# Cross-attention block on one Trainium2 core: the feed-forward as seven block products in two passes over F

## The reference, cut to what matters

```python
def _forward(query, context, wq, wk, wv, bq, bk, bv, wo, bo, ln1_g, ln1_b, ln2_g, ln2_b, w1, b1, w2, b2):
    ...
    o = jnp.einsum('bhqk,bkhd->bqhd', probs, vh).reshape(Bq, Sq, Dm)
    attn_out = o @ wo + bo
    x = query + attn_out
    h = _layer_norm(x, ln2_g, ln2_b)
    ff = jax.nn.gelu(h @ w1 + b1, approximate=False) @ w2 + b2
    return x + ff
```

## Time and profile before

| | |
|---|---|
| median of three runs | 3067.84 us |
| the profiled execution, its own time | 3068.4 us |
| its span, first to last instruction | 3066.7 us |
| mean granted TensorE clock | 0.989 |
| TensorE busy (matmul) | 2944.3 us, 96% |
| VectorE busy | 1517.7 us, 49% |
| ScalarE busy | 1155.7 us, 38% |
| stage b, from its first instruction at 1559 us | about 1508 us |

### The profile page before, as it was taken

How to read it: one execution, slowest core, us unless ns; L and a number is a source line. 1 busy time by engine, 2 the same in 40 slices (tenths; PEclk the granted TensorE clock), 3 DMA queues, 4 the chain that set the end, 5 groups by cost and what they waited for, 6 DMA issues and landing times. The chain is left out here.

```text
span 3066.7 us, 52560 instructions
## 1 busy us (share of the span) xinstructions
PE 2944.3 (96%) x17576; PEld 2390.1 (78%) x17576; DVE 1517.7 (49%) x4100; ACT 1155.7 (38%) x2958; POOL 459.3 (15%) x432
## 2 busy tenths in 40 slices
PE   6999999999999999999879999999999999999999
PEld 5777877777777778777768888888888888888887
DVE  4776667766677666677534333322333322333322
ACT  3665666656666655666522111111111111111111
POOL 1221122212222211222122000000000000000000
PEclk9999999999999999999979999999999999999999
DMA  5766666766676666667431111110111110111100
GB/s 134 124 118 107 108 110 109 123 115 101 116 110 115 116 114 108 107 112 116 73 112 57 42 41 41 41 41 0 41 41 41 41 41 0 41 41 41 41 28 14
DMA packets 123695, 231.89 MB, mean 76 GB/s; under 512 B 10752, under 2 KB 10752, under 8 KB 123648
## 3 DMA queue, kind: packets, MB, share of 16 engines
q1 hardware_dynamic: 123648, 231.28, 37.9%
HBM read 97.02 MB, written 33.55 MB: 43 GB/s over the span
## 5 line engine op out<-in xcount | busy, mean ns | idle before, releaser
L711 ACT ACTIVATE sm<-sm,mins 128x128 f32<-128x128 f32 (+3 forms) x1024 | 571.7, 559 | 570.0 <-DVE mins L574 567.4
L574 DVE CUSTOM_DVE_ANT_0 sm<-bank_s,mask 128x128 f32<-128x128 f32 (+3 forms) x1024 | 480.4, 488 | 419.9 <-PE bank_s L425 409.4
L1148 ACT ACTIVATE g_sb<-bank_f,b1s 128x512 f32<-128x512 f32 x256 | 176.2, 688 | 1173.0 <-PE bank_f L958 1173.0
L1060 DVE CAST g_hi<-g_sb 128x512 fp32r<-128x512 f32 x256 | 113.1, 442 | 866.2 <-ACT g_sb L1148 866.1
L437 PE MATMUL bank_t<-ident,sm 128*128 128x128 f32 x2560 | 419.1, 278 | 72.2 <-DVE pT L520 37.2
L437 PEld LDWEIGHTS bank_t<-ident,sm 128*128 128x128 f32 x2560 | 299.5, 141 | 177.1 <-issue 59.2
L956 PE MATMUL bank_f<-hT_hi,w_hi 128*128 128x512 f32 x1024 | 407.5, 398 | 1.6 <-DVE hT_lo L1054 1.6
L956 PE MATMUL bank_o<-w_hi,g_hi 128*128 128x512 f32 x1024 | 408.0, 398 | 0.0
L958 PE MATMUL bank_f<-hT_hi,w_lo 128*128 128x512 f32 x1024 | 406.7, 397 | 0.0
L957 PE MATMUL bank_f<-hT_lo,w_hi 128*128 128x512 f32 x1024 | 406.3, 397 | 0.0
L958 PE MATMUL bank_o<-w_hi,g_lo 128*128 128x512 f32 x1024 | 406.3, 397 | 0.0
(11 more groups left out here) (108 smaller groups left out, 4457.6 us busy)
## 6 DMA issues: line engine op xcount, KB each, us to landing
stack<-st_hi SPq DMA_DIRECT2D x256, 256.0 KB, 6.0
xt<-in_x SPq DMA_DIRECT2D x32, 1024.0 KB, 5.3
stack<-st_lo SPq DMA_DIRECT2D x128, 256.0 KB, 7.3
c_raw<-in_ctxT SPq DMA_DIRECT2D x64, 256.0 KB, 6.1
x_scratch<-xt SPq DMA_DIRECT2D x64, 256.0 KB, 2.0
xn<-x_scratch SPq DMA_DIRECT2D x16, 1024.0 KB, 7.7
xr<-x_scratch SPq DMA_DIRECT2D x16, 1024.0 KB, 5.6
out<-xr SPq DMA_DIRECT2D x64, 256.0 KB, 2.1
```

The costliest lines, as they stand in the source:

```text
L574: op = V.tensor_tensor_reduce(sm[:, n % SLOTS_S, off:off + w], bank_s[n % BANKS_S][:, off:off + w], mask[:, 512 - w:512], 1.0, 0.0, ALU.ad ...
L711: op = A.activation(row, row, ACT.Exp, bias=mins[:, g % 2, c:c + 1], scale=-1.0, accum_out=sums[:, g % 2, c:c + 1])
L1060: V.tensor_copy(g_hi[:, f % RING_H, :], g_sb[:, f % 2, :]).then_inc(g_hi_ok, 1)
L1148: A.activation(g_sb[:, f % 2, :], bank_f[f % 2][:], ACT.Gelu, bias=b1s[:, f:f + 1], scale=1.0).then_inc(gelu, 1)
```

## The change

The feed-forward is done in two passes over F, 1024 columns each; all 16 sequences go through the first pass, then all through the second. In a pass both products are 2 x 2 block products done with seven block multiplications (Winograd's form) in place of eight. The weight sums (S1 to S4 of w1, T1 to T4 of w2) are made once for each pass, on VectorE, in place in the loaded buffers, and split like the rest. The input's sums (T1 to T4) are made once for each sequence in the first pass; the split parts (`b_hi`, `b_lo`, together 3.67 MB for a sequence) are stored to HBM and loaded back in the second pass.

Layer 1 (`layer1`): fourteen steps a pass (`STEPS`), seven for each half `d` of the hidden rows, 12 matmuls each, with 256 moving columns. Products are partly summed by copying a bank to SBUF while the bank goes on being summed into (`copy`: P1, P5, U2, on ScalarE), then adding on VectorE (`add`: C11, C12, C22); C21 goes from the bank to gelu.

Layer 2 (`layer2`): seven products `k` with two halves `h` of 12 matmuls of 256 columns. Its left operands are blocks of gelu's output or sums of them (`a_sum`: S1 to S4, on VectorE), then rounded on ScalarE (`a_high`) and the remainder taken on VectorE (`a_low`), in two buffers by `k % 2`; `a_high(k, h)` waits for half `h` of product `k - 2`. Results go to `xr` by `sum_out` on VectorE, into banks `bank_x2`, `bank_y2`, `bank_z2`.

In the first pass `xr` is the stage's input and is stored back to the scratch tensor; in the second pass it is read again, GpSimd adds b2, and the output is stored. The transposed input goes through three banks (`x_bank`), spread over the steps 8 to 11 of layer 1, and ScalarE applies the layer norm's scale and bias while it copies them out (`x_high`), so `bias_product` goes. ScalarE's order of a first-pass body ends in a `h_high` for each operand of the next sequence between the `a_high`; VectorE's order is in the diff. The weights of the first body of a pass are split inside that body (`w1_parts`, `w2_parts`: eleven VectorE instructions for each of four units); unit 3 is loaded into the same buffer `xr` as unit 2, after it is used, and the first body's `xr` only after unit 3 is used. `at(c, OUTPUTS, i)` waits until `i + 1` sums of the sequence are done, in whichever order VectorE makes them.

```diff
@@ -839,15 +839,44 @@
...
+
+
...
+    STEPS = [(0, 0), (0, 1), (0, 2), (0, 3), (0, 4), (0, 5), (1, 0), (0, 6),
+             (1, 1), (1, 2), (1, 3), (1, 4), (1, 5), (1, 6)]
+    X_AFTER = {8: 0, 9: 1, 10: 2, 11: 3}
...
         def sem(name):
             return ctx.enter_context(nc.semaphore(name))
 
-        w1_hi = sb("w1_hi", [P, KT, F], F32R)
...
+        def g_block(d, name):
+            rows, cols = "C1 C2".split().index(name[:2]), "12".index(name[2])
+            return g[:, 4 * d + 2 * rows:4 * d + 2 * rows + 2, C * cols:C * cols + C]
...
-
-
-            body(0, True, False)
...
+        def over_batches(eng, body):
+
+            body(0, 0, True, False)
             with eng.Fori(1, B - 1) as c:
...
+                body(c, 0, False, False)
+            body(B - 1, 0, False, True)
+            body(B, 1, True, False)
+            with eng.Fori(B + 1, 2 * B - 1) as c:
+                body(c, 1, False, False)
+            body(2 * B - 1, 1, False, True)
...
+            def b_view(b, part):
+                return b_scratch[bass.ds(b, 1)].rearrange("o h p n -> (o h) p n")[part]
...
+                    sp.wait_ge(stored, c * 32 + 32)
+                sp.dma_start(xr[:], one(x_v, b)).then_inc(xr_in, 16)
...
+                if ph == 0:
+                    sp.wait_ge(b_lo_ok, at(c, T_LOW, "T4"))
+                    for part, m in enumerate((b_hi, b_lo)):
+                        sp.dma_start(b_view(b, part), m[:].rearrange("p a k s -> p (a k s)").bitcast(F32)).then_inc(b_stored, 16)
...
+                if ph == 1 and not last or ph == 0 and last:
+                    sp.wait_ge(step1, at(c, STEPS, (1, 6)))
+                    sp.wait_ge(b_stored, 32 * B)
+                    for part, m in enumerate((b_hi, b_lo)):
+                        sp.dma_start(m[:].rearrange("p a k s -> p (a k s)").bitcast(F32),
+                                     b_view(0 if ph == 0 else b + 1, part)).then_inc(b_in, 16)
...
+                for half in range(2):
+                    sp.wait_ge(summed, at(c, OUTPUTS, 5 + half))
+                    sp.dma_start(one(to, b)[:, 2 * half:2 * half + 2, :],
+                                 xr[:, 2 * half:2 * half + 2, :]).then_inc(stored, 16)
...
-            def hidden(c, f):
...
-            def output(c, f):
...
-            def bias_product(wc, bank):
...
+            def block_product(o, lh, ll, rh, rl, opens):
+
+                pe.matmul(o, lh, rh, start=opens, stop=False, skip_group_check=True)
+                pe.matmul(o, lh, rl, start=False, stop=False, skip_group_check=True)
+                return pe.matmul(o, ll, rh, start=False, stop=True, skip_group_check=True)
...
+            def layer1(c, ph, first, d, at_place):
+                if first:
+                    w_ready(4 * ph + d, S_LOW, PLACE1_A[at_place])
+                if d == 0 and ph == 0:
+                    pe.wait_ge(b_lo_ok, at(c, T_LOW, PLACE1_B[at_place]))
...
+                    pe.wait_ge(b_in, (c - B) * 32 + 32)
+                bank = bank_x[d]
+                if at_place == 0:
+                    pe.wait_ge(gelu, before(c, GELUS, (d, "C21")))
+                if at_place == 1:
+                    bank = bank_y
+                    pe.wait_ge(added, before(c, ADDS, (1, "C12")) if d == 0 else at(c, ADDS, (0, "C12")))
+                if at_place == 2:
+                    bank = bank_z
+                    pe.wait_ge(added, before(c, ADDS, (1, "C11")) if d == 0 else at(c, ADDS, (0, "C11")))
+                if at_place == 3:
+                    pe.wait_ge(copied, at(c, COPIES, (d, "P1")))
+                if at_place == 4:
+                    bank = bank_y
+                    pe.wait_ge(copied, at(c, COPIES, (d, "P5")))
+                if at_place == 5:
+                    pe.wait_ge(copied, at(c, COPIES, (d, "U2")))
+                if at_place == 6:
+                    pe.wait_ge(added, at(c, ADDS, (d, "C22")))
+                for m in range(2):
+                    cols = slice(P * (2 * d + m), P * (2 * d + m) + P)
+                    for kt in range(2):
+                        mm = block_product(bank[:, C * m:C * m + C], w1_hi[:, at_place, kt, cols],
+                                           w1_lo[:, at_place, kt, cols], b_hi[:, at_place, kt, :],
+                                           b_lo[:, at_place, kt, :], at_place < 3 and m == 0 and kt == 0)
+                mm.then_inc(step1, 1)
...
+            def layer2(c, ph, first, k):
+                bank = bank_x2
+                if k == 0:
+                    pe.wait_ge(summed, before(c, OUTPUTS, 6))
+                if k == 1:
+                    bank = bank_y2
+                    pe.wait_ge(summed, before(c, OUTPUTS, 5))
+                if k == 2:
+                    pe.wait_ge(summed, at(c, OUTPUTS, 0))
+                if k == 3:
+                    bank = bank_z2
+                    pe.wait_ge(summed, before(c, OUTPUTS, 3))
+                if k == 4:
+                    pe.wait_ge(summed, at(c, OUTPUTS, 2))
+                if k == 5:
+                    bank = bank_y2
+                    pe.wait_ge(summed, at(c, OUTPUTS, 1))
+                if k == 6:
+                    pe.wait_ge(summed, at(c, OUTPUTS, 4))
+                for h in range(2):
+                    if first:
+                        w_ready(4 * ph + 2 + h, T_LOW, PLACE2_B[k])
+                    pe.wait_ge(a_lo_ok, at(c, A_LOW, (k, h)))
+                    for kt in (2 * h, 2 * h + 1):
+                        for t in range(2):
+                            rows = slice(P * t, P * t + P)
+                            mm = block_product(bank[:, C * t:C * t + C], a_hi[:, k % 2, kt, rows],
+                                               a_lo[:, k % 2, kt, rows], w2_hi[:, k, kt, :], w2_lo[:, k, kt, :],
+                                               k in (0, 1, 3) and kt == 0 and t == 0)
+                    mm.then_inc(step2, 1)
...
+            def body(c, ph, first, last):
+                for n, (d, place) in enumerate(STEPS):
+                    if n == 13:
+                        layer2(c, ph, first, 0)
+                    layer1(c, ph, first, d, place)
+                    if n in X_AFTER and ph == 0 and not last:
+                        f = X_AFTER[n]
...
+                        x_transpose(c + 1, f, x_bank(f))
+                if ph == 0 and not last:
+                    pe.wait_ge(hT_ok, c * KT + KT + 3)
+                for k in range(1, 7):
+                    layer2(c, ph, first, k)
+
+            over_batches(pe, body)
...
+            def add(c, d, name):
+
+                place, bank, copy = {"C11": (2, bank_z, "P1"), "C12": (4, bank_y, "U2"), "C22": (5, bank_x[d], "P5")}[name]
+                dve.wait_ge(copied, at(c, COPIES, (d, copy)))
+                dve.wait_ge(step1, at(c, STEPS, (d, place)))
+                V.tensor_tensor(g_block(d, name), bank[:].rearrange("p (m s) -> p m s", m=2), g_block(d, name),
+                                ALU.add).then_inc(added, 1)
...
+            def a_low(c, k, h):
+                dve.wait_ge(a_hi_ok, at(c, A_HIGH, (k, h)))
+                low(a_part(a_lo, k, h), a_source(k, h), a_part(a_hi, k, h), a_lo_ok)
...
+                if ph == 0:
+                    h_parts(c, 4)
+                if first:
+                    w1_parts(U + 1, 1, 0)
+                if norm:
                     for t in range(QT):
-                        x_low(c + 1, t)
...
+                add(c, 0, "C11")
+                if norm:
+                    normalise(c + 1, 0)
+                    normalise(c + 1, 1)
...
+                add(c, 0, "C12")
+                a_low(c, 0, 0)
+                if norm:
+                    normalise(c + 1, 2)
+                    normalise(c + 1, 3)
+                add(c, 0, "C22")
...
+                a_sum(c, "S1", 0)
+                a_low(c, 1, 0)
+                a_sum(c, "S2", 0)
...
+                add(c, 1, "C11")
...
+                add(c, 1, "C12")
+                a_low(c, 0, 1)
...
+                add(c, 1, "C22")
...
+                a_sum(c, "S1", 1)
+                a_low(c, 1, 1)
...
+                a_sum(c, "S2", 1)
+                sum_out(c, ph, 0)
+                a_low(c, 2, 0)
+                a_low(c, 2, 1)
+                a_sum(c, "S3", 0)
+                a_sum(c, "S3", 1)
+                a_sum(c, "S4", 0)
+                a_low(c, 3, 0)
+                a_sum(c, "S4", 1)
+                a_low(c, 3, 1)
+                if norm:
+                    h_parts(c + 1, 0)
...
+                a_low(c, 4, 0)
+                sum_out(c, ph, 2)
+                a_low(c, 4, 1)
+                if norm:
+                    h_parts(c + 1, 1)
...
+                a_low(c, 5, 0)
+                sum_out(c, ph, 1)
+                a_low(c, 5, 1)
+                sum_out(c, ph, 3)
+                if norm:
+                    h_parts(c + 1, 2)
+                a_low(c, 6, 0)
...
+                a_low(c, 6, 1)
+                sum_out(c, ph, 4)
```

(4 more changed lines are left out.)

645 lines of the change are left out of this document (426 added, 219 removed).

## The result

| | before | after |
|---|---|---|
| median of five runs | 3068.71 us (3067.33 to 3070.71) | 3084.26 us (3083.22 to 3085.45) |
| span of the profiled execution | 3066.7 us | 3081.5 us |
| ratio | | 1.0052, 95% interval 1.004 to 1.0063 |

The change makes the kernel slower, by 16 us (0.5%). The forecast was 3052.4, faster: wrong in sign, 32 us off, with the measured time inside the range of 3012 to 3092. Two steps of it failed: the distance between matmuls of 256 columns, taken from stage a, and the queue of stores and loads in the first body.

A forecast was written before the change was run, and what follows sets the result against it. TensorE's rate was the bound. First body's end 1667, 14 first-pass bodies at 46.65, then 45.8, 55.4, 15 second-pass bodies at 41.7 and 4.5 gave span 3051, forecast 3052.4 us; 8-in-10 range 3012 to 3092.

The forecast's parts named there:

- first second-pass body: First body of the second pass: 33 more VectorE instructions, 19.8 us, of which 14.7 stick out; 55.4 us, plus or minus 5.
- The rate: TensorE's 256-column matmuls in stage b: 0.1183 us each, from a stage a row of twelve; bounds 0.1168 and 0.136.
- The rival for the rate: 256-column matmuls slower in long runs than in twelves: at 0.136 each, 190 us more, 3242; chance 0.05.
- The first body: First pass's first body: ends at 1667, plus or minus 5; store queued behind xr's load, only h_high waiting for it.
- The clock: Half clock after the long wait in about every second first-pass body: 1.0 us a body on average, bounds 0 and 3.5.
- The wait at k = 4: Layer 2, TensorE waits for VectorE's third output sum: 3.8 us in a first-pass body, 0.94 in a second-pass body.
- Front: Start of a first-pass body: VectorE late at C11 makes step 5 0.3 late, C22 0.1 more; 0.4 us.
- b2: Second pass: GpSimd's additions slow VectorE's subtractions, so step 12 starts about 1.0 us late; bounds 0 and 1.5.
- The reload of `b_hi` and `b_lo`: Second-pass loads: landed at 35 us, wanted at 41, free; a late-reload rival had 3.6 us a body, 3106, chance 0.05.
- The heavier clock: Clock falls at every long wait for 7 us or more: 37 more, 3090; chance 0.25 shared with VectorE at 0.66.
- The lighter case: Clock stays up and b2's additions meet nothing: 14 and 15 us less, about 3023; chance 0.18.
- The full gain: VectorE is not late at k = 4 in layer 2: 2950 us; chance 0.05.

The follow-up runs named there:

- e1_halves: The kernel before, with every 512-column product of its feed-forward issued as two of 256 columns: 3099.1 us, ratio 1.0096.
- e14_store: The changed kernel, with the first body's store of b_hi and b_lo issued behind the load of unit 2: 3073.2 us, ratio 1.0013 on before.
- e9: The changed kernel, with the work for the next sequence put behind the layer 2 parts in first-pass bodies: 3020.6 us, ratio 0.9841 on before.
- e13: e11 with the two loops of a layer 1 step exchanged: 2967.6 us, ratio 0.9676 on before.
- e15_all: e11 with the early first store of e14_store added: 2957.2 us, ratio 0.9635 on before.
- e11: The changed kernel with waits on the right sums, next-sequence parts behind layer 2, b2 held back, and VectorE's front additions moved earlier: 2968.1 us.
- e4_no_b2: The changed kernel without GpSimd's additions of b2 in the second pass: 3066.8 us, ratio 0.9993 on before.
- e2_widths: The kernel before, with 512-column products issued in pieces of varying widths, read for matmul distances only: one run, 4789.2 us.

## Why the prediction was wrong, point by point

The span was forecast at 3051 and measured at 3081.5. By the terms of the sum:

| term | forecast | measured | number | us more |
|---|---|---|---|---|
| end of the first body | 1667 | 1674.84 | 1 | 7.8 |
| first-pass body | 46.65 | 47.29 (mean) | 14 | 9.0 |
| 16th body | 45.8 | 47.39 | 1 | 1.6 |
| first second-pass body | 55.4 | 57.96 | 1 | 2.6 |
| second-pass body | 41.7 | 42.36 (mean) | 15 | 9.9 |
| after the last sum | 4.5 | 3.9 | 1 | -0.6 |

**The rate, mis-sized.** 0.1183 was taken from one row of twelve in stage a, "of the same form". In stage b it is 0.1200. The bounds given were 0.1168 and 0.136, and the likeliest value was put at the row; the difference of 0.0017 looks small, but it stands under 10752 matmuls: 18 of the 30 us, 0.57 in every body. With 0.1200 in the sum the forecast is 3070, no change, and the sign hangs on the rest. The row itself was fair: in the kernel before, all 64 such rows of twelve at full clock have 0.1178 to 0.1189, with a mean of 0.1186, which would have moved the forecast by 3 us. What failed was to carry the distance from one stage to the other. e1_halves shows that the half length has a price in stage b with nothing else changed: 30.5 us, 0.1193 on average and 0.1200 in layer 2. The rest, 0.0007 x 10752 = 8 us, has no cause shown. The rival for the rate had the right direction, with a price of 190 us from the mean time of a weight load, and the wrong condition: long rows are not slower than short ones. Nothing lay between it and the row of twelve. That rate should have been a continuous term with a range of its own, not a rival with a chance of 0.05. The Trainium skill, "TensorE: Matmul & The Clock Gate", section "Back-to-back issue gap", has 262 cycles, 109 ns, for 256 columns, and calls it the gap of a single matmul, without the loads. With a load for each, the runs have 117 to 120, and that figure would have made the miss larger.

**The first body, a step that failed.** The prediction said of the store of `b_hi` and `b_lo` that it is queued on SyncE behind the load of `xr` and that only `h_high` waits for it, 24 us in. That is right for a later body, where `xr` is loaded at the start. In the first body the same `xr` stands behind unit 3 and lands at 1642.9 (forecast 1644), the store behind it at 1651.6, and ScalarE, in order, does not come to `a_high(2, 1)`. The queue was read once, for the steady state, and not again for the body in which what stands ahead of it is late. e14_store shows the cause. From first to last sum 20.8 and 2 for the clock were forecast; 32.0 were measured, and 22.0 with the store moved. That the first sum itself was so near is luck: the first product of the stage started at 1584.47, forecast about 1590, and the stretch from it to the first sum took 58.4 us, forecast 54. (The prediction's own terms give 1622.4 where it writes 1624.) Where these 4 us went was not followed.

**The clock, mis-sized a little.** Forecast: a fall in every second first-pass body, 1.0 us a body on average. Measured: in 12 of 14, half clock for 3.4 us, 1.5 us each (47.50 less 46.02), 1.3 on average. The falls are bound to the long waits: none in the 14 bodies of e9 to e13 and of e15, where no wait is longer than 1.04. In the 16th body half clock lasted 6.8 us, of which 5.0 lay behind the end of a wait of 4.8; that is most of its 1.6.

**What held.** The wait at k = 4 in the first pass: 3.54, forecast 3.8. In the second: 0.91, forecast 0.94. Each costs 0.10 more than its length, which the forecast did not have. Transposes 1.73, forecast 1.7. Front 0.3 (46.02 less 3.64 less 42.05), forecast 0.4; e11 shows it as VectorE's. b2: 1.03 a body, forecast 1.0, by three instructions of 1.05, 1.43 and 1.78 beside GpSimd. The rule of the Trainium skill, "SBUF — State Buffer", section "Who interferes with whom", is borne out by these rows, and by the add out of PSUM that kept its 0.69; held back, the additions ran from 2540.9 and met a subtraction that has cover (1.65), which is why holding them back is enough. The reload of `b_hi` and `b_lo` (7.4 and 11.1 us to landing) made nobody wait. The first second-pass body was 2.6 over; 0.6 is the rate, and by e4_no_b2 (56.25 against 57.96) 1.7 is b2. The forecast's 55.4 is 39.75 + 14.7 and about 0.95: it holds the wait at k = 4 or b2, not both. The rest was not followed.

**The rivals.** The heavier clock was half right: the fall came at nearly every long wait, but lasted 3.4 us and not 7, and its price (3.5 a fall) was too high. The lighter case fell: no cost was missing. The full gain, 2950, was the time without waits at k = 4; it takes off 2 us of clock a body where the sum had 1.0, so by its own terms it is 2965. That e15_all, without waits outside the first bodies and at 0.1200, is at 2957 is no confirmation of it: it has other edits too. The sum had margins of 15 us on a saving of 161 of which 145 were to go to waits and the first bodies: a forecast of the sign on such a margin was less sure than 0.65.

**What stays open.** Why the distance is 0.1200 in every product of the changed stage b, 0.1186 in stage a and 0.1174 to 0.1200 in e1_halves. Order of the three matmuls and half of the bank are excluded, and longer rows are not slower; where the operands lie in SBUF was not tried. What decides whether a wait of 3.5 us brings the clock down (12 of 14) was not tried either.

## What to carry to other kernels

Where the bound is a rate and the edit changes the form of the instruction, a row from another stage is a sample, not the rate: 1.5% of error in it was larger than the margin of the whole forecast. More rows of that stage would not have helped, since all 64 lie between 0.1178 and 0.1189. Changing the form alone, in the place where it will stand, would have: e1_halves needs nothing of the change and gives 0.1200 in layer 2. When an order is walked, walk the first body and each queue in it again by itself, since what is free in the steady state (a store behind a load) can stand behind a late load there.

A wait that is removed is worth what is late next: the same 0.91 us at k = 4 was worth 1.0 in the second pass and 0.08 in the first, until the front was reordered. The gain of 127 us from the changed kernel to e15_all came from order and waits alone, with the same block products: take work for the next sequence out of the stretch in which TensorE waits for this one's, and count which sum a wait really needs.

## What the runs showed of the hardware

In e2_widths, matmuls with a weight load each stand about 0.11 us apart at full clock, whether they have 64, 128 or 192 columns; an eighth of the 512-column distance would be 0.029 for 64 columns. At half clock (1.2 GHz) the distance is 0.427 at 512 columns, which is 512 columns at that clock, and 0.213 at 64, 128, 192 and 256; at full clock (2.4 GHz) 512 columns take 0.2337, 10% more than half of 0.427. So the half clock costs a factor of 1.83 at 512 columns and 1.78 at 256 (against 0.1200), not 2.

In e2_widths the granted clock stood at half in stretches of 64-column matmuls although TensorE issued without a pause, also in the 8 us before each such fall (mostly matmuls of 128 and 64 columns, no idle time). One such stretch by its busy times, clock 0.50:

```profile
3900.00:3910.00 10.00, 10.00 (x49) 10.00 (x48) 0.00 (x0) 0.00 (x0) 0.00 (x0) 0.50 0.00 0
```

I had not expected this: the fall of the earlier trace rows stood behind products of one column, in which TensorE did next to nothing. A fall behind a wait of 3.5 us lasted 3.4 us and cost 1.5, less than half of the bound of 3.5 that the prediction kept.
